# Spreading the last stage's matrix products over all of its units, with twelve left for behind the last one

## The reference

```python
h = sigmoid(einsum('bts,st->bs', x, W1) + b1)     # x: 1024 x 24 x 1024, W1: 1024 x 24
y = h @ W2.T + b2                                 # W2: 1024 x 1024, all float32
```

## Time and profile before

| | |
|---|---|
| median of 3 runs (lowest, highest) | 319.12 us (318.98, 320.89) |
| the profiled execution | 320.03 us, span of its instructions 318.2 us |
| mean granted TensorE clock | 0.949 |
| busy, share of the span | TensorE 84%, VectorE 78%, GpSimd 68%, ScalarE 16% |
| loads and stores | 109.48 MB, mean 344 GB/s |

### The profile page before, as it was taken

One profiled execution on the slowest core, in us unless ns is written; L12 is line 12 of the kernel. 1 busy time (PEld: TensorE's weight loads), 2 busy tenths in 40 slices (PEclk: granted clock), 3 DMA queues, 4 the chain that ended last, 5 costly groups with the idle time before them and its releaser, 6 DMA issues.

```text
span 318.2 us, 4779 instructions
## 1 busy us (share of the span) xinstructions
PE 266.2 (84%) x1761; PEld 229.1 (72%) x1761; DVE 247.8 (78%) x368; ACT 50.9 (16%) x85; POOL 215.1 (68%) x125
## 2 busy tenths in 40 slices
PE   0957769478879999997799999589999959999594
PEld 0856659378758888887788887478888848888373
DVE  0729998549989888889869887967878985779925
ACT  4201214102270110010600000130111040000300
POOL 2219656555479999984999876499888589981000
PEclk9979999959999999999799999959999998999878
DMA  7999999999999999999999999999999999887007
GB/s 232 402 388 387 386 386 386 401 387 387 386 386 385 387 386 386 387 382 378 374 374 377 382 385 385 384 373 374 373 373 370 363 345 299 260 262 233 2 2 265
DMA packets 67675, 109.48 MB, mean 344 GB/s; under 512 B 3642, under 2 KB 40514, under 8 KB 67652
## 3 DMA queue, kind: packets, MB, share of 16 engines
q1 hardware_dynamic: 67056, 107.06, 94.5%
q10 hardware_dynamic: 596, 2.11, 1.6%
HBM read 104.97 MB, written 4.19 MB: 343 GB/s over the span
## 4 chain that ended last, share of the span: by engine, by line
PE 56%; DMA 29%; DVE 5%; issue 5%; ACT 2%; SPq 1%; DVEq 0%; ACTq 0%
DMA ring<-in_r_x 29%; PE xbank L227 27%; PE pbank L296 22%; DVE acc L346 3%; PE xbank L324 3%; PE pbank L324 1%; PE pbank L286 1%; DVE w_lo L353 1%; ACT h L421 1%; PE pbank L256 1%; ACT h_hi L446 1%; PE pbank L245 0%; DVE acc L344 0%; ACT L421 0%; SPq L190 0%
## 5 line engine op out<-in xcount | busy, mean ns | idle before, releaser
L346 DVE SCALAR_TENSOR_TENSOR acc<-xbank,w,acc 128x512 f32<-128x512 f32 x280 | 200.7, 746 | 45.1 <-PE xbank L227 37.3
L227 PE MATMUL xbank<-ident,ring 128*128 128x128 f32 x1184 | 175.8, 286 | 41.7 <-DMA ring<-in_r_x 35.2
L227 PEld LDWEIGHTS xbank<-ident,ring 128*128 128x128 f32 x1184 | 147.8, 148 | 71.2 <-issue 27.7
L475 POOL TENSOR_TENSOR nat<-nat,w1all 128x768 f32<-128x768 f32 (+2 forms) x56 | 107.0, 1912 | 60.6 <-DMA nat<-in_r_x 47.8
L485 POOL TENSOR_TENSOR nat<-nat 128x768 f32<-128x768 f32 (+2 forms) x46 | 87.7, 1906 | 3.6
L296 PE MATMUL pbank<-w_lo,h_hi 128*128 128x512 f32 x112 | 48.5, 433 | 0.0
L296 PE MATMUL pbank<-w_hi,h_hi 128*128 128x512 f32 x112 | 48.5, 433 | 0.0
L296 PE MATMUL pbank<-w_hi,h_lo 128*128 128x512 f32 x112 | 39.7, 427 | 0.0
L421 ACT ACTIVATE h<-acc,b1col 128x512 f32<-128x512 f32 (+1 forms) x22 | 12.5, 599 | 102.0 <-DVE acc L346 102.0
L340 DVE TENSOR_SCALAR acc<-xbank,w 128x512 f32<-128x512 f32 x16 | 12.0, 749 | 13.8 <-PE xbank L227 11.8
L296 PEld LDWEIGHTS pbank<-w_hi,h_hi 128*128 128x128 f32 x112 | 21.7, 194 | 0.9
(11 more groups left out here) (37 smaller groups left out, 98.8 us busy)
## 6 DMA issues: line engine op xcount, KB each, us to landing
ring<-in_r_x SPq DMA_DIRECT2D x38, 1024.0 KB, 13.3
ring<-in_r_x SPq DMA_DIRECT2D x36, 768.0 KB, 11.0
nat<-in_r_x SPq DMA_DIRECT2D x20, 512.0 KB, 13.1
nat<-in_r_x SPq DMA_DIRECT2D x24, 384.0 KB, 11.5
ring<-in_r_x SPq DMA_DIRECT2D x18, 512.0 KB, 5.2
y<-in_L_rec_W SPq DMA_DIRECT2D x2, 2048.0 KB, 15.0
nat<-in_r_x SPq DMA_DIRECT2D x12, 256.0 KB, 8.3
out_y<-y ACTq DMA_DIRECT2D x4, 512.0 KB, 6.5
```

The lines of the kernel that those rows point to most:

```text
L227: mm = pe.transpose(xbank[u % XBANKS][:, j * P:(j + 1) * P], tile, ident[:, :])
L346: nc.vector.scalar_tensor_tensor(out=total, in0=bank, scalar=weight, in1=total, op0=ALU.mult, op1=ALU.add).then_inc(unit_added, 1)
L475: nc.gpsimd.tensor_tensor(slot, slot, row, ALU.mult).then_inc(nat_weighed, 1)
```

## The change

Only stage 4 is touched, and what follows it. (1) `steps_due` of the last stage: the first step comes behind unit 2, and 60 of the 72 steps are spread evenly, 5 for every 3 units, up to the last unit. (2) The remaining 12 (`REST`) stand behind the last unit and ahead of the stage's own products. (3) VectorE's `add_out` of tiles 6 and 7 of stage 3 come behind its `h_hi`/`h_lo` pieces. (4) The own products use the six `xbank` for tiles 0 to 5 and the two `pbank` for tiles 6 and 7; before, tiles 0 and 1 had the `pbank`.

```diff
+    REST = 12
...
         def steps_due(i, v):
 
             steps = OUTS * steps_of(i - 1)
+            if i == LAST:
+                lead = chunks[i]
+                return max(0, -(-(v - lead + 1) * (steps - REST) // (len(units[i]) - lead)))
             lead = 2 * chunks[i]
-            span = len(units[i]) * (4 if i < LAST else 3) // 5 - lead
+            span = len(units[i]) * 4 // 5 - lead
             return max(0, min(steps, -(-(v - lead + 1) * steps // span)))
...
+            last_steps = OUTS * steps_of(LAST - 1)
+            for k in range(last_steps - REST, last_steps):
+                product_step(LAST - 1, k)
             for c in range(chunks[LAST]):
                 for n in range(OUTS):
                     j, cols = out_half(n)
-                    if c == 0 and n < 2:
-                        pe.wait_ge(y_added, added_at[LAST] - 1 + n)
-                    if c == 0 and n >= 2:
-                        pe.wait_ge(unit_added, UNITS - XBANKS + n - 2 + 1)
+                    if c == 0 and n < XBANKS:
+                        pe.wait_ge(unit_added, UNITS - XBANKS + n + 1)
+                    if c == 0 and n >= XBANKS:
+                        pe.wait_ge(y_added, added_at[LAST] - OUTS + n + 1)
                     if n % OH == 0:
                         pe.wait_ge(tail_lo, c * JT + j + 1)
-                    bank = pbank[n] if n < 2 else xbank[(UNITS + n - 2) % XBANKS]
+                    bank = xbank[(UNITS + n) % XBANKS] if n < XBANKS else pbank[n - XBANKS]
...
+            for n in range(outs_due(LAST, len(units[LAST]) - 2), OUTS):
+                add_out(LAST - 1, n, pbank[n % 2])
             for n in range(OUTS):
-                add_out(LAST, n, pbank[n] if n < 2 else xbank[(UNITS + n - 2) % XBANKS])
+                add_out(LAST, n, xbank[(UNITS + n) % XBANKS] if n < XBANKS else pbank[n - XBANKS])
```

## The result

The changed kernel takes 315.52 us (315.15 to 316.05, 4 runs) against 319.22 us (318.98 to 320.89): a ratio of 0.9885, interval 0.9854 to 0.9917, so 3.7 us less. Run again later beside an experiment it had 315.77 us. The forecast was 310.0 us with a range of 308.2 to 314.0: the sign was right, but of the 9.2 us that it promised the change brought 3.7.

What follows compares the result with a forecast made beforehand. Loads, TensorE and VectorE were taken to set the pace in turns. 294.2 to the own products + 10.85 for them + 4.05 for the end = 309.1 us of span against 318.2; forecast time 310.0 us, range 308.2 to 314.

Steps and rivals of the forecast that it cites:

- TensorE's chain through the changed stage: Stage 4 from 261.79 us: 34 units and 68 products, 30.8 us plus 1.64 for the clock; last product ends at 294.2.
- GpSimd and the loads as cover: Late stage 4: GpSimd's last sum (286.2) and the loads (done at 287.3) come just in time; both covers called thin.
- 2.4 us of cover: End of stage 4's loads: all bytes in at 287.3 us, the last t needed at about 289.7.
- 1.64 us dip: Start of t = 8: the low clock makes the first two units take 4.35 us, not 2.71; kept whole in the sum.
- The prediction's own sign of being wrong: Stage 4: TensorE waiting for `ring` or GpSimd's sum near 286 us was among the signs that would refute the forecast.
- They hide behind VectorE's last units and the sigmoid: End of stage 4: the 12 products, 2.7 us, fit where TensorE had stood idle for 3.7 us.
- the clock: Own products at the end: full clock from the start, 10.85 us in place of 13.96, 3.1 us of the gain.
- The four early products: Behind units 2 and 3, up to 261.79 us: they lie in the wait for t = 8, cost 0.
- VectorE's stall: Behind unit 7, near 267 us: VectorE idle once for about 2 us, as the first `add_out` needs the 15th step.
- its chain to 293.0: VectorE in stage 4: 23.7 us of adds from 269.1, last unit added at 293.0, nearly no slack.
- the loads get no faster: Rival for stage 4's loads: the last t still lands only at 295.36, time 315.4 us; chance 0.09.
- The clock never oscillated: Rival for stage 4: short waits drop the clock, 27.9 us over the whole stage; 319 us and more, chance 0.04.

Runs made afterwards that it cites:

- e6_halfnat: Changed kernel with each of the ten `nat` loads of stage 4 bringing one of its two blocks of 128 rows: 314.07 us.
- e9_fill: Changed kernel with its 60 products behind units 2 to 25 and the first `add_out` behind unit 11 in place of 7: 311.99 us.
- e2_slot: Changed kernel with chunk 0 of stage 4 in the free slot, so ScalarE no longer waits for stage 3's last product: 314.09 us.
- e5_span30: Changed kernel with all 72 products spread evenly behind units 2 to 30, none left behind the last unit: 315.06 us.
- e1_rest0: Changed kernel with all 72 products spread up to the last unit, none left behind it: 313.87 us.
- e3_addout: Changed kernel with the first `add_out` behind unit 11 in place of unit 7: 315.54 us.
- e4_rest_only: Changed kernel with its 60 products behind units 4 to 21, as densely as before the change, and 12 at the end: 316.08 us.
- e11_changed: The changed kernel measured again, unaltered, on another chip: 315.77 us.
- e7: Changed kernel with 58 products behind units 2 to 25, 14 behind the last 12, `add_out` 0 later, ScalarE's wait moved to VectorE: 311.96 us.
- e8: As e7, with the last two `nat` loads issued ahead of t = 19 and 21 in place of 18 and 19: 311.96 us.

## Why the prediction was wrong

**The step that failed is "TensorE's chain through the changed stage", with its cover in "GpSimd and the loads as cover".** I summed TensorE's work from t = 8 to the last unit as if it never waited, and tested the loads against it with one number, the time by which *all* bytes are in (287.3). The bulk came about as computed: the rate falls behind 287 us, 287.3 and the 0.8 us of shift being 288.1. But the very last load, issued at 284.2 once t = 18 had been turned, landed at 290.35, so even for the last t the 2.4 us of cover were not there (TensorE came to it late, at 293.31, and didn't wait). And the test was at the wrong place. The `nat` loads all lie ahead of t = 19, so t = 9 to 19 carry 11 x 0.524 + 8 x 0.262 = 7.86 MB and the last four t only 2.1. These loads took 22.33 us, 2.0 us per t up to t = 19. (That would be 352 GB/s, above the window's 335; part of them was already under way when t = 8 landed.) TensorE's work there is 22 x 0.455 + 36 x 0.225 = 18.1 us, 1.65 per t. Checked at t = 19 instead of at the end, the cover was negative by 4.2 us at full clock. Against my chain with its 1.64 us dip, 19.75, TensorE came to unit 26 2.6 us late; e6_halfnat moves it by the bytes taken out, e9_fill gives the time back by putting products there. The prediction's own sign of being wrong, TensorE waiting for `ring`, is in the timeline.

**The second is that the wait in ScalarE's program was overlooked.** "They hide behind VectorE's last units and the sigmoid" is the sentence that was wrong: the sigmoid waits for them. From the last turn's end (294.22 + 0.44, what a turn takes) to the own products I had 3.15 us and it took 4.35; e2_slot takes the 1.22 us of idle time out.

The account of the spans, from the forecast's 9.1 us: 2.6 for t = 8 to t = 19; 0.2 for t = 19 to the last turn (9.7 us for 9.5); 1.2 for ScalarE; 0.3 and 0.1 for the own products (299.01 to 310.17, 11.16 for 10.85) and the stores; 0.8 for the shift ahead of stage 4, which no step of the prediction covers and no run explains. 9.1 - 5.2 = 3.9, the difference of the spans.

**Right:** the clock. I had the 12 products keep it up at the end for 3.1 us; it was granted 1.00 from the first own product, and the stretch to the end is 2.7 us shorter. e5_span30 leaves TensorE idle there and pays 1.4 us of it again. Products spread up to the last unit do the same as the block of 12 (e1_rest0). The dip at t = 8, which I kept in the sum, went: 1.0 us of idle time and not 2.13. The 1.64 us that I had for it are inside the 2.6 above; without them the miss up to t = 19 is 4.2 us. The four early products cost nothing. VectorE's stall was sized right (2.25 us for "about 2"), but its chain to 293.0 didn't bound anything (e3_addout). `add_out` 6 and 7 held nothing up.

**The rivals.** The time met "the loads get no faster", 315.4 us, by chance; that mechanism didn't occur, 335 GB/s against 271. The clock never oscillated: 1.00 in every window from 254 to 310 us, with TensorE waiting 0.45 to 0.98 us for six of its loads. The Trainium skill's page "TensorE: Matmul & The Clock Gate", section "A second HAM failure mode: psum-queue depth-cycling", tells of a kernel whose clock oscillates as TensorE idles briefly and often between groups of matmuls that cycle through PSUM banks; in this kernel that isn't seen, by the 1.00 of those windows.

Open stays why stage 4 starts up to 1.5 us later in some executions.

## What to carry to other kernels

Test a cover at every point where the resource is consumed, not at the end: the bytes up to that point against the work up to it. When a row names the releaser of a wait, check when that releaser was done. Filler work belongs where the engine waits; spread evenly over a stage that is first load-bound and then engine-bound, it is partly kept for the wrong half (e9_fill, 3.8 us). When work is moved behind a point, look up every wait on its semaphore in all engines' programs, also those that cost nothing before, since a trace doesn't show them.

## What the runs showed of the hardware

- After 2.13 us of idle time at t = 8 (before) the granted clock was 0.53 in 261.8 to 265.4 us, after 2.04 us (e4_rest_only) 0.79 in 262 to 266 us. After 0.91 to 1.08 us at the same place it stayed at 1.00. Ahead of the own products, 3.7 and 3.2 us of idle time were followed by matmuls at 0.43 us, 1.2 us by matmuls at 0.23.
- The length of the idle stretch alone doesn't decide. Near 153 us every kernel runs the same program, and in ten of the twelve traces TensorE stands still there for 2.0 to 2.2 us. In the 2.5 us behind that stretch the clock was 0.57, 0.64, 0.63 and 0.77 after 2.17, 2.19, 2.16 and 2.17 us (before, changed, e11_changed, e4_rest_only) and 1.00 after 2.18, 2.02, 2.19, 2.13, 2.15 and 2.05 us (e2, e3, e5, e7, e8, e9). At 209.4 us of e2_slot it was 1.00 even after 3.54 us, where the kernel before has 0.50 after 3.56 us. After the stretches of 1.0 to 1.9 us behind 150 us it was 1.00 each time.
- In the changed kernel's windows from 256 to 286 us the loads of stage 4, with rows of 1 KB, run at 331 to 349 GB/s at a share of 1.03 to 1.09. In the trace of before those of stages 2 and 3, with rows of 1.5 KB, have 371 to 373 in 160 to 174 and 216 to 250 us, and those of stage 1, with rows of 2 KB, 386 in 100 to 130 us, at shares of 1.05 to 1.06. By these rates the loads of the last stage need some 10% more time for the same bytes (an estimate, 373 over 340).
